# A graph network's three edge passes: one-hots built four at a time on VectorE, transposed one-hots on ScalarE, waits dropped

## The reference, cut to what matters

```
m = segment_max(logits, dst)              # one maximum per node (and head)
a = exp(logits - m[dst])
out = segment_sum(values[src] * a, dst)   # and the sum of a, for the denominator
```

## Time and profile before

| | |
|---|---|
| median of 3 runs | 4923.0 us (4912.32 to 4923.89) |
| the profiled execution's own time | 4959.05 us |
| its span in the profile | 4957.4 us, mean granted TensorE clock 0.788 |
| GAT, attention, typed pass (first gather to last addition) | about 253 to 1525, 1730 to 3035, 3231 to 4507 us |
| busy over the whole span | TensorE 67%, VectorE 65%, GpSimd 59%, ScalarE 46% |
| DMA | 118 GB/s mean |

### The profile page before, as it was taken

The page is one execution under the profiler, slowest core; times in us unless marked ns, Lnnn a source line. Parts: engine busy times, 40 slices in busy tenths (PEclk is TensorE's granted clock), DMA queues, the critical chain, the costliest instruction groups (busy, mean ns, idle before and its releaser), DMA issues. The chain is left out here.

```text
span 4957.4 us, 74006 instructions
## 1 busy us (share of the span) xinstructions
PE 3333.3 (67%) x13766; PEld 2197.6 (44%) x13766; DVE 3239.2 (65%) x11427; ACT 2269.2 (46%) x6293; POOL 2911.1 (59%) x3158
## 2 busy tenths in 40 slices
PE   0536666766676657777777777836667666765998
PEld 0424444434443434444444444523444444434887
DVE  4546666666667946665656566847777777776665
ACT  0224555555553335555555555525545545553332
POOL 1266666666662456666666662366666666661776
PEclk9956766576668978898888889967676676677999
DMA  5345444544442334444434433544444444441221
GB/s 54 107 133 146 143 141 140 149 140 141 141 143 67 115 101 113 112 114 113 112 113 117 114 113 103 190 135 132 130 133 133 135 132 130 133 131 55 63 68 49
DMA packets 313472, 586.81 MB, mean 118 GB/s; under 512 B 106395, under 2 KB 204231, under 8 KB 313111
## 3 DMA queue, kind: packets, MB, share of 16 engines
q0 software_dynamic: 122944, 354.78, 26.1%
q1 hardware_dynamic: 147832, 188.48, 13.3%
q10 hardware_dynamic: 42336, 39.66, 2.3%
HBM read 504.91 MB, written 77.73 MB: 118 GB/s over the span
## 5 line engine op out<-in xcount | busy, mean ns | idle before, releaser
L561 PE MATMUL psum<-big,onehot 128*128 128x264 f32 (+2 forms) x4992 | 2149.5, 547 | 842.1 <-DVE big L733 312.8
L561 PEld LDWEIGHTS psum<-big,onehot 128*128 128x128 f32 x4992 | 1063.4, 253 | 1225.0 <-issue 675.2
L755 DVE TENSOR_TENSOR acc<-acc,psum 128x264 f32 (+2 forms) x2496 | 1051.3, 421 | 595.2 <-PE psum L561 372.0
L446 POOL DMA_INDIRECT big<-table_attn,tables x832 | 787.7, 947 | 499.8 <-PE psum L561 189.2
L446 POOL DMA_INDIRECT big<-table_gat,tables x832 | 841.1, 1011 | 403.8 <-issue 205.2
L446 POOL DMA_INDIRECT big<-table_typed,tables x832 | 816.7, 982 | 429.5 <-issue 215.3
L472 ACT ACTIVATE dist<-iota,tables 128x128 f32<-128x128 f32 x2496 | 1000.0, 401 | 101.2 <-DMA tables<-edge_tables 14.3
L484 ACT ACTIVATE onehot<-dist,ones 128x128 f32<-128x128 f32 x1664 | 649.6, 391 | 854.1 <-PE psum L561 552.5
L518 PE MATMUL psum<-big,onehot_t 128*128 x2496 | 484.6, 308 | 239.0 <-issue 144.7
L597 DVE CUSTOM_DVE_ANT_0 junk<-psum,big 128x258 f32<-128x258 f32 x832 | 344.6, 415 | 323.7 <-DMA joins<-visit_joins 174.4
L481 ACT ACTIVATE onehot<-dist,weight,neg_weight 128x128 f32<-128x128 f32 x832 | 400.4, 482 | 318.9 <-PE psum L561 184.4
(11 more groups left out here) (251 smaller groups left out, 3625.9 us busy)
## 6 DMA issues: line engine op xcount, KB each, us to landing
onehot_t<-onehots SPq DMA_DIRECT2D x104, 512.0 KB
big<-visit_positions SPq DMA_DIRECT2D x52, 512.0 KB
onehots<-onehot_t SPq DMA_DIRECT2D x52, 512.0 KB
seg<-visit_segments SPq DMA_DIRECT2D x676, 24.1 KB
big<-table_gat,tables POOLq DMA_INDIRECT x832
big<-table_attn,tables POOLq DMA_INDIRECT x832
big<-table_typed,tables POOLq DMA_INDIRECT x832
big<-in_x_dram SPq DMA_DIRECT2D x98, 128.0 KB
```

Source lines behind the costliest of these rows:

```text
L446: pool.indirect_dma_start(X[:, v % RING, :], None, ph.table, bass.IndirectOffsetOnAxis(ap=column(k, 0)[:, g:g + 1].bitcast(I32), axis=0)). ...
L561: nc.tensor.matmul(sum_ps(v), m.onehot[:, v % 4, :], X[:, v % RING, 0:ph.WS], start=True, stop=True).then_inc(S["summed"], 1)
L755: nc.vector.tensor_tensor(row, row, sum_ps(v), ALU.add).then_inc(S["added"], 1)
```

## The change

1. GAT and typed passes: ScalarE's `distance` and `onehot` are gone. VectorE compares a row of 0..127 with the positions of four visits in one operation (`onehots`, 128 x 512 elements) ahead of `scale_rows(v)` for each v divisible by 4, into eight slots. The operation has no semaphore of its own.
2. TensorE's wait for a visit is `scaled` alone in these passes. `scale_rows(v)` itself now waits until the addition of visit v - 4 is complete, and the additions no longer wait for each other, but for those at a batch's start and the last three.
3. The transposed one-hots of the GAT pass move to ScalarE, as two activations over 128 x 2048 (`Abs`, in place, then `Relu`), placed in ScalarE's own order behind `weigh`.
4. Attention pass: `distance` is made one visit ahead instead of three, and waits for the addition of the visit four before its own (so `distance(v + 1)`, which ScalarE does before `onehot(v)`, waits for the addition of visit v - 3). TensorE then waits for the one-hot alone, but at the last visit. The dot products rotate over three scratch rows instead of two and drop two waits.

```diff
+    def onehot_at(v):
+        return m.onehots[:, v % 4, :] if ph.dot else m.onehots[:, v % 8, :]
...
             def load_tables(k):
                 if k >= TB:
-                    sp.wait_ge(S["distance"], (k + 1 - TB) * G)
+                    if ph.dot:
+                        sp.wait_ge(S["distance"], (k + 1 - TB) * G)
...
             def distance(v):
-                if v >= 4:
-                    act.wait_ge(S["onehot"], v - 3)
+                if v >= SB + 1:
+                    act.wait_ge(S["added"], v - SB)
...
             def onehot(v):
                 act.wait_ge(S["distance"], v + 1)
-                if v >= 4:
-                    act.wait_ge(S["summed"], v - 3)
...
+            def transposed_onehot(k):
+                act.wait_ge(S[f"positions{k % 2}"], (k // 2 + 1) * 16)
+                at = m.rel_row.bitcast(BF16)[:, k % 2, :]
+                nc.scalar.activation(at, at, ACT.Abs, scale=-1.0, bias=m.pcol[:, 0:1]).then_inc(S["spacing"], 1)
+                act.wait_ge(S["spacing"], k + 1)
+                if k >= 2:
+                    act.wait_ge(S["expanded"], k - 1)
+                    act.wait_ge(S[f"onehot_stored{k % 2}"], k // 2 * 16)
+                nc.scalar.activation(m.onehot_t[:, k % 2, :], at, ACT.Relu, scale=-1.0, bias=m.ones[:, 0:1]).then_inc(S["onehot_t"], 1)
...
-            for v in range(-LEAD, VISIT_END):
-                if 0 <= v + 3 < VISIT_END and v + 3 >= 0:
-                    distance(v + 3)
-                if v >= 0:
+            for v in range(-3 * G, VISIT_END):
+                if ph.dot and 0 <= v + 1 < VISIT_END:
+                    distance(v + 1)
+                if ph.dot and v >= 0:
                     onehot(v)
                 k, g = batch_at(v)
                 if k is not None and g == weigh_at:
                     weigh(k)
+                if ph.name == "gat" and v % G == 2 and 0 <= v // G + 2 < NBATCH:
+                    transposed_onehot(v // G + 2)
...
                 if v >= 0:
-                    pe.wait_ge(S["onehot"], v + 1)
-                    if not ph.dot:
-                        pe.wait_ge(S["scaled"], v + 1)
-                    if v >= SB:
+                    pe.wait_ge(S["onehot" if ph.dot else "scaled"], v + 1)
+                    if ph.dot and v == VISIT_END - 1:
                         pe.wait_ge(S["added"], v + 1 - SB)
...
+            def onehots(v):
+                k, g = divmod(v, G)
+                nc.vector.tensor_tensor(m.onehots[:, v % 8:v % 8 + 4, :], m.iota[:, :].unsqueeze(1).to_broadcast([P, 4, P]), spread(column(k, 1)[:, g:g + 4], P), ALU.is_equal)
...
             def dot(v):
                 dve.wait_ge(S["expanded"], v + 1)
-                landed(dve, v)
-                if v >= 2:
-                    dve.wait_ge(S["dotted"], v - 1)
+                if v % QUARTER == 0:
+                    landed(dve, v)
...
             def scale_rows(v):
+                if v >= 4:
+                    dve.wait_ge(S["added"], v - 3)
...
             def add(v, blk):
                 if v % G == 0:
                     dve.wait_ge(S["rescaled"], v // G + 1)
-                else:
+                elif ph.dot or v >= VISIT_END - 3:
                     dve.wait_ge(S["added"], v)
...
+                    if (v + 2) % 4 == 0:
+                        onehots(v + 2)
                     scale_rows(v + 2)
...
-                if ph.name == "gat" and v % G == 2 and 0 <= v // G + 2 < NBATCH:
-                    transposed_onehot(v // G + 2)
```

More of the change, by code:

```diff
@@ L477, in onehot @@
                 act.wait_ge(S["distance"], v + 1)
-                if v >= 4:
-                    act.wait_ge(S["summed"], v - 3)
-                if ph.dot:
-                    nc.scalar.activation(m.onehot[:, v % 4, :], m.dist[:, v % 4, :], ACT.Relu,
-                                         scale=m.neg_weight[:, k % 2, g:g + 1], bias=m.weight[:, k % 2, g:g + 1]).then_inc(S["onehot"], 1)
-                else:
-                    nc.scalar.activation(m.onehot[:, v % 4, :], m.dist[:, v % 4, :], ACT.Relu,
-                                         scale=-1.0, bias=m.ones[:, 0:1]).then_inc(S["onehot"], 1)
+                nc.scalar.activation(m.onehots[:, v % 4, :], m.dist[:, v % 4, :], ACT.Relu,
+                                     scale=m.neg_weight[:, k % 2, g:g + 1], bias=m.weight[:, k % 2, g:g + 1]).then_inc(S["onehot"], 1)
+            def transposed_onehot(k):
[7 more added lines that the diff above has]
+                nc.scalar.activation(m.onehot_t[:, k % 2, :], at, ACT.Relu, scale=-1.0, bias=m.ones[:, 0:1]).then_inc(S["onehot_t"], 1)
             weigh_at = G - 1 if ph.dot else G - 2
-            for v in range(-LEAD, VISIT_END):
-                if 0 <= v + 3 < VISIT_END and v + 3 >= 0:
-                    distance(v + 3)
-                if v >= 0:
+            for v in range(-3 * G, VISIT_END):
+                if ph.dot and 0 <= v + 1 < VISIT_END:
+                    distance(v + 1)
+                if ph.dot and v >= 0:
                     onehot(v)
@@ L555, in _ @@
                 if v >= 0:
-                    pe.wait_ge(S["onehot"], v + 1)
-                    if not ph.dot:
-                        pe.wait_ge(S["scaled"], v + 1)
-                    if v >= SB:
+                    pe.wait_ge(S["onehot" if ph.dot else "scaled"], v + 1)
+                    if ph.dot and v == VISIT_END - 1:
                         pe.wait_ge(S["added"], v + 1 - SB)
-                    nc.tensor.matmul(sum_ps(v), m.onehot[:, v % 4, :], X[:, v % RING, 0:ph.WS], start=True, stop=True).then_inc(S["summed"], 1)
+                    nc.tensor.matmul(sum_ps(v), onehot_at(v), X[:, v % RING, 0:ph.WS], start=True, stop=True).then_inc(S["summed"], 1)
                 k, g = batch_at(v)
@@ L580, in blocks_of @@
                     skip_runtime_bounds_check_because="visits() keeps them within the blocks")[1]
-            def transposed_onehot(k):
-                dve.wait_ge(S[f"positions{k % 2}"], (k // 2 + 1) * 16)
-                if k >= 2:
-                    dve.wait_ge(S["expanded"], k - 1)
-                    dve.wait_ge(S[f"onehot_stored{k % 2}"], k // 2 * 16)
-                nc.vector.tensor_scalar(m.onehot_t[:, k % 2, :], m.rel_row.bitcast(BF16)[:, k % 2, :],
-                                        m.pcol[:, 0:1], None, ALU.is_equal).then_inc(S["onehot_t"], 1)
+            def onehots(v):
+                k, g = divmod(v, G)
+                nc.vector.tensor_tensor(m.onehots[:, v % 8:v % 8 + 4, :], m.iota[:, :].unsqueeze(1).to_broadcast([P, 4, P]), spread(column(k, 1)[:, g:g + 4], P), ALU.is_equal)
             def dot(v):
                 dve.wait_ge(S["expanded"], v + 1)
-                landed(dve, v)
-                if v >= 2:
-                    dve.wait_ge(S["dotted"], v - 1)
+                if v % QUARTER == 0:
+                    landed(dve, v)
                 if v % G == 0 and v:
                     dve.wait_ge(S["logits"], v // G)
-                nc.vector.tensor_tensor_reduce(out=m.junk[:, v % 2, 0:K], in0=ps[:, exp_banks[v % 3], 0:K], in1=X[:, v % RING, 0:K], scale=1.0,
+                nc.vector.tensor_tensor_reduce(out=m.junk[:, v % 3, 0:K], in0=ps[:, exp_banks[v % 3], 0:K], in1=X[:, v % RING, 0:K], scale=1.0,
                                                scalar=0.0, op0=ALU.mult, op1=ALU.add,
@@ L1727, in build_program @@
         m.onehot_t = sb("onehot_t", [P, 2, G * P], BF16)
-        m.onehot, m.dist = sb("onehot", [P, 4, P]), sb("dist", [P, 4, P])
+        m.onehots = sb("onehots_or_distances", [P, 8, P])
+        m.dist = m.onehots[:, 4:8, :]
         m.raw, m.logit, m.shifted = sb("raw", [P, P]), sb("logit", [P, P]), sb("shifted", [P, P])
@@ L1736, in build_program @@
         m.weight, m.neg_weight = sb("weight", [P, 2, G]), sb("neg_weight", [P, 2, G])
-        m.junk = sb("junk", [P, 2, WQ])
+        m.junk = sb("junk", [P, 3, WQ])
         m.psum = ctx.enter_context(nc.psum_tensor("psum", [P, 8, 512], F32))
```

## The result

The change made the kernel slightly faster: 4891.66 us (median of 6, 4883.98 to 4899.03) against 4918.35 us for the kernel before on the same chip (median of 6), a ratio of 0.9947 with an interval of 0.9933 to 0.9961. The forecast of 4959 us had the wrong sign.

A forecast was written before the change was run, and what follows sets the result against it. The prediction took gathers and their late completions to pace all three passes. Terms 20 + 3 - 6 + 15 + 4 = 36 us on the 4923 us median gave 4959 us, own range 4938 to 5000, wide range 4870 to 5090.

The forecast's parts named there:

- The gathers, and the late completions that come with them: All three passes: GpSimd's gathers and TensorE completions arriving late during them set the pace, 1.484 to 1.520 us a visit.
- 1% and 7%: Shares of added work expected to show: about 1% for VectorE in GAT and typed passes, 7% for waits in the loop.
- The signs of being wrong: Attention pace beyond 1.6 us, GAT or typed pace moving by more than 0.03 us either way, or longer gathers.
- The attention pass, +15 us: Attention pass: matmul 0.87 us behind the addition instead of 0.12; 208 us if all shows, 7% taken, 15 us slower.
- ScalarE out of the loop, -6 us: GAT and typed passes: visit 15's wait for its one-hot behind `weigh` goes; 73 and some 20 us, 7% counted.
- Terms 3, -6 and 4 us: VectorE's added work before the last gathers, ScalarE out of the loop, and gathers lengthened beside the new operation.
- the rival "Faster": Fewer matmul signals and no ScalarE delay at visit 15 show fully: 4853 us, or 4900 with half; chance 0.26.
- bound of 73 us: Typed pass: most that ending visit 15's wait could save, 1.4 us in each of 52 batches.
- The tails, 20 us: Behind the last gather of the GAT and typed passes, one-hots and exposed waits on VectorE cost 10 us a pass.
- VectorE, 3 of 280 us: GAT and typed passes, 49 batches before the last gather: 280 us more VectorE work, of which 3 us appears.
- The rival in which VectorE becomes the limit: VectorE rises to about 1.14 and 1.27 us a visit; if half of 280 us shows, 5096 us; chance 0.08.
- Gathers beside the new operation, +4 us: GAT and typed passes: one-hots on VectorE lengthen GpSimd's gathers; 37 us in proportion, a tenth taken.

The follow-up runs named there:

- the chain alone: Kernel before with only the attention pass's new distance chain, dot-product waits as before: 0.9996 of the kernel before, on a prompt chip.
- the swapped order: Changed kernel with the 128x512 one-hot operation right behind the scaling instead of ahead of the next: 0.9971 (late chip), 0.9994 (prompt chip) of the kernel before.
- the four operations of one input: Changed kernel with four 128x128 one-hot operations of one SBUF input replacing each 128x512 of two: 0.9968 (late chip), 0.9977 (prompt chip) of the kernel before.
- the first experiment: Kernel before with only the attention pass's edits (new distance chain, fewer TensorE and dot-product waits), on a prompt chip: 1.0012 of the kernel before.

## Why the prediction was wrong

*What paces the passes.* "The gathers, and the late completions that come with them" fits as a description of late chips, and the traces of before came from one: completions are late while gathers are issued, and no longer behind the last one. That the gathers cause it was not tested there; they don't by themselves, since on prompt chips the same gathers delay none. One trace could not show that. What failed is the use made of it: I took the pace as fixed to 1% and 7%, and let only the shown fractions of added work through. But the waits in that pace are part of the loop, and a change of the order of waits moves them. All three passes got 1.1 to 1.4% faster per visit on a late chip (16.2, 13.0 and 14.1 us by the table). The signs of being wrong that the prediction named came true: the GAT pace moved by 0.036 us by the profiles, gathers of the typed pass got longer (984 to 1021 ns), and the attention pace fell to 1.486 us instead of rising to 1.52 or more.

*The attention pass, +15 us: this step had the wrong sign.* It measured -13 us (0.9972 against 0.9998, visits 1186.9 against 1200.9). The step's own mechanism is there. Timeline of the changed kernel, addition, distance, one-hot, weights:

```profile
2419.86 0.42 DVE L762 TENSOR_TENSOR acc<-acc,psum 128x258 f32 x1
...
2420.31 0.40 ACT L477 ACTIVATE onehots_or_distances<-iota,tables 128x128 f32<-128x128 f32 x1 [2.34 <-issue]
2420.61 0.48 ACT L483 ACTIVATE onehots_or_distances<-onehots_or_distances,weight,neg_weight 128x128 f32<-128x128 f32 x1
...
2421.14 0.30 PEld L570 LDWEIGHTS psum<-big,onehots_or_distances 128*128 128x128 f32 x2 [0.71 <-ACT onehots_or_distances L483]
```

The matmul comes 2421.14 - 2420.28 = 0.86 us behind the addition, where I had 0.87. But it isn't on the path of a prompt chip, where the chain alone is 0.9996; on a late one, whatever it costs is outweighed, for the part gains. The 7% shown was a guess from another loop. What gains the 13 us, the chain or the dropped waits of the dot products, is open, since the run that separates them came to a prompt chip.

*ScalarE out of the loop, -6 us, and the loops of the other two passes as a whole.* Terms 3, -6 and 4 us make +1; by the table it was -30 us for these visits on a late chip. The measured sum for everything but the attention part is -1 us (0.9998, -5 to +3), with 18 us of tails and 6 us between the passes in it, so some 25 us of gain in the visits, which agrees. This term was mis-sized, on the side of the rival "Faster": I gave it 93 us or half. (Its bound of 73 us counts 1.4 us a batch where the lines give 1.48, so 77.) Which of one signal instead of three, ScalarE's delay at visit 15 and the moved transposed operation brings it on late chips was not told apart; those runs fell on prompt chips.

*The tails, 20 us: right.* 41.4 to 50.5 and 44.5 to 53.3 us, 9 each. The one-hot operation takes 0.675 us (0.67 expected), the scaling's wait 0.45 - 0.34 = 0.11 us a visit (0.12). The Trainium skill ("VectorE: DVE Perf Modes", The DRAIN you can't avoid) would make that wait free; the timeline disagrees where the semaphore waited for is that of the operation just ahead.

*VectorE, 3 of 280 us: right in kind.* 0.985 to 1.129 us a visit, pace shorter. The rival in which VectorE becomes the limit has nothing for it.

*Gathers beside the new operation, +4 us: the term that decides on prompt chips.* I had 37 us by proportion and took a tenth. On late chips gathers do grow (1018 to 1026, 984 to 1021 ns) and it costs nothing, since GpSimd waits that much less. On prompt chips, where nothing hides a gather, the GAT gathers of 1.057 us cost 1071.6 - 1021.2 = 50 us against the swapped order. There the proportion isn't the rule at all; what VectorE does at a gather's start, and what follows it, is. The shared ports of the Trainium skill ("SBUF — State Buffer", SBUF: two separate sides) fit a gather that stands while VectorE reads two SBUF inputs, and fit that it doesn't beside an operation that reads PSUM. Why a gather is held past the end of the operation that it met first, and why the four operations of one input did no better than the swap (1.003 against 0.997 us), they don't explain. The bf16 operation holds single gathers too (30 that began beside it on a prompt chip took 1.46 to 1.48 us, in the first experiment), though doubled on a late chip it left the mean as it was (1.014 against 1.012 us).

*Not foreseen:* 6 us in the stretch from GAT's last addition to the attention pass's first gather, whose code is unchanged: 204.9 and 204.7 us with the GAT pass of before, 211.1 and 211.4 after. It comes with the transposed move: that part alone has 211.4 and 212.3 us, the one-hots alone 205.3 and 205.2. But the version with one input has the move and 203.8 and 204.6 us, so the cause is open.

## What to carry to other kernels

When an engine idles on waits in a pace, don't multiply added work by a fraction "shown" and call the pace fixed: ask for each dropped or added wait whether it is in the loop that frees the buffers, and give it its own price in both signs. Profile the kernel before on more than one chip before a half-percent change is judged, for the same program had two different limits here. Where a GpSimd queue is the clock, look at which VectorE operations stand at the start of its long instructions, and try their order before their number: a swap of two lines was worth 0.8% on prompt chips, and nothing on a late one.

## What the runs showed that was not expected

- Two kinds of chip for one program: 4909 to 4953 us, with matmul completions up to 28 us late while gathers are issued, and 4436 to 4442 us, with 0.05 us at the same place. The mean granted clock of a run is 0.79 to 0.80 on the first and 0.85 to 0.86 on the second.
- A gather of 0.95 us alone took 1.83 us with a step of the segment maximum at its start and VectorE's one-hots and scaling begun 0.34 us into it, and 0.95 us with an addition from PSUM at its start and the same two operations begun 0.08 or 0.35 us into it. VectorE's operations kept their length (0.68 and 0.41 us).
- Three parts of 1.0006, 0.9981 and 0.9967 made 1.0075 together.
